# Three PSUM banks instead of two for the up projections of a mixture of experts

## What is computed

```python
x = x + ga * attention(layernorm(x) * (1 + ca) + sa)
h = layernorm(x) * (1 + cb) + sb

def ffn(xt):                                   # xt: the 2048 rows of h
    ew, ei = top_k(xt @ gate_w, 2)
    ew = softmax(ew)
    wE = sum(ew * (ei == each expert))         # (8, tokens), two weights per token
    hid = gelu(einsum('td,edf->etf', xt, w1) + b1)     # 8 experts, 128 -> 256
    o = einsum('etf,efd->etd', hid, w2) + b2           # 256 -> 128
    y = layernorm(xt + o, ln_g, ln_b)                  # one norm per expert
    return einsum('et,etd->td', wE, y)

x = x + gb * ffn(h)
```

## Time and profile before

| | before |
|---|---|
| timed runs, us | 268.58, 270.12, 270.11; median 270.11 |
| profiled execution, us | 268.45, of which 266.7 from the first to the last instruction |
| busy, share of the span | PE 88%, PEld 76%, DVE 69%, ACT 60%, POOL 51% |
| mean granted TensorE clock | 0.976 of full speed |
| the Gelus (line 484) | 128 ACTIVATEs, 50.4 us busy, 472 ns each |

### The profile page before, as it was taken

The page is one execution under the profiler, slowest core; times in us unless marked ns, Lnnn a source line. Parts: engine busy times, 40 slices in busy tenths (PEclk is TensorE's granted clock), DMA queues, the critical chain, the costliest instruction groups (busy, mean ns, idle before and its releaser), DMA issues.

```text
span 266.7 us, 7792 instructions
## 1 busy us (share of the span) xinstructions
PE 235.2 (88%) x3064; PEld 201.8 (76%) x3064; DVE 183.2 (69%) x570; ACT 159.4 (60%) x419; POOL 134.7 (51%) x254
## 2 busy tenths in 40 slices
PE   7796889998999999999999899998999999989970
PEld 3455468887888888888888788887888888858960
DVE  2989858485866677686967587677858595455175
ACT  2454408836695648744893759654884479356650
POOL 8082655247713674266714771367525660378075
PEclk9996899999999999999999999999999999999995
DMA  7930000000000000000000000000000000000000
GB/s 199 366 140 2 2 2 0 2 4 4 0 20 6 0 2 20 4 2 4 20 2 2 0 2 21 5 2 2 20 2 2 2 21 2 4 0 0 22 0 21
DMA packets 5652, 6.23 MB, mean 23 GB/s; under 512 B 336, under 2 KB 5104, under 8 KB 5360
## 3 DMA queue, kind: packets, MB, share of 16 engines
q1 hardware_dynamic: 5616, 5.74, 6.7%
HBM read 4.68 MB, written 1.05 MB: 21 GB/s over the span
## 4 chain that ended last, share of the span: by engine, by line
PE 47%; DVE 24%; ACT 16%; POOL 7%; issue 5%; POOLq 0%; ACTq 0%; DVEq 0%
ACT hid L484 11%; PE z L1003 6%; PE turns L867 6%; PE score L974 6%; DVE q_st L590 6%; PE score L966 5%; ACT L445 3%; DVE ypart L660 3%; PE turns L869 3%; PE turns L868 3%; DVE xn L570 3%; PE score L985 3%; PE score L1048 2%; POOL rstd L340 2%; ACT prob L445 2%
## 5 line engine op out<-in xcount | busy, mean ns | idle before, releaser
L484 ACT ACTIVATE hid<-turns,pack_ffn 128x256 f32<-128x256 f32 x128 | 50.4, 472 | 39.3 <-PE turns L869 39.3
L1003 PEld LDWEIGHTS z<-w,hid 128*128 128x128 f32 x480 | 59.4, 191 | 3.7 <-issue 1.0
L1003 PE MATMUL z<-w,hid 128*128 128x128 f32 x480 | 61.5, 276 | 0.0
L309 POOL TENSOR_SCALAR zvar<-zss 128x4 f32<-128x4 f32 x32 | 6.2, 193 | 78.4 <-DVE zss L646 69.4
L323 POOL TENSOR_TENSOR ypart<-ypart 128x256 f32<-128x256 f32 (+1 forms) x60 | 36.0, 600 | 18.4 <-DVE ypart L660 15.4
L867 PE MATMUL turns<-h_hi,w_hi 128*128 128x256 f32 x128 | 39.7, 310 | 5.0 <-ACT hid L484 4.8
L868 PE MATMUL turns<-h_lo,w_hi 128*128 128x256 f32 x128 | 35.9, 280 | 0.0
L869 PE MATMUL turns<-h_hi,w_lo 128*128 128x256 f32 x128 | 35.9, 280 | 0.0
L660 DVE SCALAR_TENSOR_TENSOR ypart<-z,zcoef,ln_gG 128x128 f32<-128x128 f32 x120 | 34.1, 341 | 1.8 <-POOL zcoef L314 1.7
L310 POOL TENSOR_TENSOR zrstd<-zvar,mhalf 128x4 f32<-128x4 f32 x32 | 33.1, 1033 | 2.7
L867 PEld LDWEIGHTS turns<-h_hi,w_hi 128*128 128x128 f32 x128 | 24.0, 188 | 9.8 <-ACT hid L484 9.5
(11 more groups left out here) (143 smaller groups left out, 454.7 us busy)
## 6 DMA issues: line engine op xcount, KB each, us to landing
w<-in_w SPq DMA_DIRECT2D x2, 1024.0 KB, 7.2
out_x<-yout SPq DMA_DIRECT2D x8, 128.0 KB, 1.8
x_tokens<-in_x SPq DMA_DIRECT2D x1, 896.0 KB, 6.7
ln_g<-in_ln_g SPq DMA_DIRECT2D x1, 512.0 KB
pack_mod<-in_pack_mod SPq DMA_DIRECT2D x1, 385.0 KB, 3.0
pack_proj<-in_pack_proj SPq DMA_DIRECT2D x1, 193.0 KB, 4.3
pack_att<-in_pack_att SPq DMA_DIRECT2D x1, 130.5 KB, 4.2
x_tokens<-in_x SPq DMA_DIRECT2D x1, 128.0 KB, 2.9
```

The costliest lines, as they stand in the source:

```text
L484: last = a.activation(hid[:, e, c, :], U[(e + 1) % 2][:, c * STEP:(c + 1) * STEP], ACT.Gelu, bias=b1[:, e, c:c + 1])
L1003: last = mm(z_bank(f, q)[:, e * D:(e + 1) * D], hid[:, ee, c, tt * P:(tt + 1) * P], w2[:, ee * CH + c, :], start=False, stop=e == HALF - 1 ...
```

## The change

The up projections and the Gelus go round three banks: U[1], U[0] and zB[0], so that up 0, 3 and 6 write U[1], up 1, 4 and 7 write U[0], and up 2 and 5 write zB[0]. In the last step S[0] stands in place of zB[0]. From e = 3 on, up e waits for Gelu e - 3. Up 2 waits until its bank is free of its last reader: in the first step of the sum of biases that was made at the start, in the later ones of the scaling of z 2 of the step before (`u_done`), in the last step of the attention (`x1_s`). z 0, which uses zB[0] again, now also waits for Gelu 5, save in the last step. The first use of U[1] and U[0] in a step, and the last, are by the same experts as before.

The instructions on each engine, and their order, are the same in both kernels.

```diff
+        def up_bank(i, e):
+
+            return (U[1], U[0], S[0] if i == STEPS - 1 else zB[0])[e % 3]
...
                 for c in range(CH):
-                    last = a.activation(hid[:, e, c, :], U[(e + 1) % 2][:, c * STEP:(c + 1) * STEP], ACT.Gelu,
+                    last = a.activation(hid[:, e, c, :], up_bank(i, e)[:, c * STEP:(c + 1) * STEP], ACT.Gelu,
                                         bias=b1[:, e, c:c + 1])
                 last.then_inc(gelu_s, 1)
...
                 if e == 1:
                     pe.wait_ge(g_out, i + 1)
-                if e > 1:
-                    pe.wait_ge(gelu_s, 8 * i + e - 1)
+                if e == 2 and i == STEPS - 1:
+                    pe.wait_ge(x1_s, i + 1)
+                elif e == 2 and i > 0:
+                    pe.wait_ge(u_done, 4 * i - 1)
+                elif e == 2:
+                    pe.wait_ge(bias_o_s, 1)
+                if e > 2:
+                    pe.wait_ge(gelu_s, 8 * i + e - 2)
                 for c in range(CH):
-                    last = three(U[(e + 1) % 2][:, c * STEP:(c + 1) * STEP], w1_hi[:, e, c, :], w1_lo[:, e, c, :],
+                    last = three(up_bank(i, e)[:, c * STEP:(c + 1) * STEP], w1_hi[:, e, c, :], w1_lo[:, e, c, :],
                                  h2_hi[:, i % 2, :], h2_lo[:, i % 2, :])
                 last.then_inc(up_done, 1)
...
                 half, tt = q // 2, q % 2
                 pe.wait_ge(gelu_s, 8 * f + HALF * (half + 1))
+                if f < STEPS - 1 and q == 0:
+                    pe.wait_ge(gelu_s, 8 * f + 6)
```

## The result

The changed kernel took 259.0 us in the median of four runs (257.99, 258.18, 259.82 and 259.93), the kernel before 270.04 beside it (268.58 to 270.12). The ratio is 0.960, with a 95% interval from 0.955 to 0.965: 4% faster. The profiled execution took 257.99 us, 256.2 of it span, against 268.45 and 266.7. The code has become longer at the top, so line 484 is now 488, 867 to 869 are 871 to 873, 974 is 984 and 1003 is 1013.

A forecast was written before the change was run, and what follows sets the result against it. The round of two banks, with TensorE and ScalarE taking turns, was taken as the bound; 7 x 1.33 + 0.99 = 10.30 us, and 269.28 - 10.30 = 259.0 us, range 257.5 to 262.4 us.

The forecast's parts named there:

- The mechanism: Up projections and Gelus: with two banks, up 2 waits for Gelu 0 and Gelu 2 for up 2; gaps of 0.33 us.
- The stage: Gelus of each of the first seven steps: sixteen ACTIVATEs without a gap, 5.95 us in place of 7.28.
- 1.33 per step: Each of the first seven steps: Gelus end 1.33 us sooner, and all of it reaches the next step.
- 0.99 in the last step: Last issue of up 1 to first down projection: 2.96 us at TensorE's pace in place of 3.95, 0.99 less.
- What was priced at nothing: New TensorE waits: up 2 for VectorE's scaling of z, 0.64 us to spare, and down projections for Gelu 5; no cost.
- The level: Timed runs fall on two levels 1.66 us apart: forecast 258.15 and 259.81 us, with the middle taken, 259.0.
- One gap left: Rival: one of three Gelu gaps stays in each of the seven steps, 7.22 us gained, 262.1 us; chance 0.10.
- TensorE as the bound: Rival: TensorE is the bound and only its matmuls' 4.8 us of waiting for Gelus goes, 264.5 us; chance 0.06.
- Given back to VectorE: Rival: the next step waits for VectorE's subtractions, so earlier Gelus gain nothing, 269.3 us; chance 0.03.
- The clock: Rival: the longer gap before the transposes lowers TensorE's clock, 3.0 us in each of seven steps, 280.0 us; chance 0.03.
- Were it 0.25 us shorter, VectorE would be next: VectorE's wait for the small exponential: 1.33 of 1.58 us goes, 0.25 stays as the cover that hides its work.
- TensorE and not ScalarE sets the last step's pace: Last step from up 5 on: down projections stand between the last ups, so TensorE sets the pace.

The follow-up runs named there:

- the kernel with the waits of two: The changed kernel with its three banks, but each up projection from up 2 on again waits for Gelu e-2; 270.49 us, ratio to before 1.003.
- the kernel with two products: The changed kernel without the up projections' product of h with the low part of w1, four matmuls per expert in place of six; 256.62 us, 0.951.
- the kernel with both made quicker: The changed kernel without the product with the low part of w1 and without b1, so one Gelu ACTIVATE per expert; 248.73 us, 0.922.

## Why the prediction was right, and where its steps were not

**The mechanism.** That two banks made TensorE and ScalarE take turns is shown from both sides: the third bank without the later waits gives back all gaps and the time, one wait gives back one gap.

**The terms.** The stage was forecast at 5.95 us and measured 5.96; 1.33 per step against (202.19 - 192.74) / 7 = 1.35; 0.99 in the last step against 1.00, with 2.96 from the last issue of up 1 to the down projection, as worked out. The sum was 10.30, the span lost 10.5 and the profiled execution 10.46. The 0.02 per step that the sum lacks lies in the stage's own two sizes: the Gelus end 5.94 us after the first begins (100.78 - 94.84) and not 5.95, and before they took 7.28 to 7.30 us in the seven steps, of which the sum took the shortest.

**What was priced at nothing** did cost nothing: up 2's wait had 0.63 us to spare (forecast 0.64), the idle time ahead of the transposes is 0.52 (0.53), and 0.24 is left of VectorE's wait (0.25).

**The level.** Both levels came out, 257.99 and 258.18 against 258.15, and 259.82 and 259.93 against 259.81. That two of the four runs fell on each level, so that their median is the forecast middle, is luck: with all four near the upper level, as when the changed kernel ran again, it is 259.4.

**The rivals.** One gap left cost 0.53 per step when it was put back, not 0.44, and did not occur. TensorE as the bound is refuted by the kernel with a third fewer matmuls in the stage, but it is only 0.02 us per expert behind: with a quicker ScalarE it is the bound at once. Given back to VectorE did not happen. The clock stayed at 1.00 in the stage, with stops and without, and in the window of the longer gap. The fall by which that rival was priced did not come again at its place either: in the changed kernel TensorE stood idle for 1.68 us ahead of 22.22, and the windows from 20 to 26 show 1.00. The Trainium skill, page "TensorE: Matmul & The Clock Gate", section "A second HAM failure mode: psum-queue depth-cycling", says that short stops between groups of matmuls that go round PSUM banks make the clock swing; neither kernel shows it in the Gelu stage, before with 23 such stops.

**The step that failed.** "Were it 0.25 us shorter, VectorE would be next" is wrong. Extra work of 1.2 us cost 0.16 per step, so the cover there is about 1.04. The 0.24 was only the first wait on VectorE's row; behind it TensorE takes the weights 0.76 us after they are ready. I had read the cover off the waiting engine's own idle time and not off the engine that waits for its result.

**True by a little** is that TensorE and not ScalarE sets the last step's pace. Gelu 3 ends there at 235.15 and the down projection that needs it starts at 235.50, so TensorE is 0.35 us from being stopped by ScalarE; I had used the statement as if it held for any pace, and with shorter ups the step gained 0.6 where TensorE's alone would have given 1.9.

## What to carry to other kernels

When two engines hand PSUM banks to each other, compare the round trip of all banks (work of both and the two hand-overs) with the slower engine's own pace times the number of banks (here 1.90 us against 2 x 0.73 with two banks): a gap of the same length at every round, and waits of each engine for the other in like number, show that one more bank is worth the gap, up to the slower engine's own pace. A bank that another stage uses will do, if its last reader is done before the round gets there. How much an engine may still grow is read from the consumer of its results, not from its own idle time.

## What the runs showed that was not expected

**A second semaphore on a matmul.** In both kernels in which up 2 waits for two semaphores at once, and the Gelu is the later one, the gap ahead of Gelu 2 is 0.40 us, not 0.33, and the table of waits of the kernel with the waits of two has a row that the kernel before lacks:

```profile
PEld z L871 <- issue: 3.4, 7, 0.5
```

Once in each of seven steps, and its step is 29.14 in place of 29.07. It is not the z bank: in the last step of both kernels up 2 writes S[0], also with two semaphores, and the gap is 0.40 and 0.41. That the second semaphore is the cause was argued from this and not tested by itself.

**TensorE's pace in the first ten microseconds decides the level.** In the thirteen traces here the first Gelu starts either between 39.4 and 39.9 or between 40.6 and 41.1. TensorE's timeline ahead of it, of the changed kernel's first trace

```profile
5.83 1.14 PE L897 MATMUL z<-pack_mod,silu 128*128 128x128 f32 x8
```

and of its second

```profile
6.64 2.05 PE L897 MATMUL z<-pack_mod,silu 128*128 128x128 f32 x8
```

The eight matmuls ahead of these start at 4.94 in both and take 1.02 and 1.84 us. By line 917 (8.87 and 10.20) the second trace is 1.33 us late, and about that it stays up to the first Gelu. All traces fall in line: the same eight matmuls take 1.14 us in the six with the early first Gelu and 2.05 or 2.06 in the seven with the late one. That it is the 1.2 GHz level that makes them slow is argued: the second trace's record of the clock begins only at 12.67, and its windows ahead of that show 1.00 for want of one. But line 917 takes 1.06 us in both traces there, in the first inside the window from 8 to 12 with a clock of 0.57, and 0.70 us later, in windows with 1.00. Why the start is slow in some executions stays open.

**VectorE stood behind GpSimd.** In the first step of the kernel with two products, on VectorE

```profile
41.33 2.79 DVE L701 TENSOR_TENSOR gdif<-gtop 128x2 f32<-128x2 f32 x1
```

and on GpSimd

```profile
41.31 0.45 POOL L367 TENSOR_TENSOR ln_bG<-ln_b,gates 8x128 f32<-8x128 f32 x1
41.73 2.38 POOL L366 TENSOR_TENSOR ln_gG<-ln_g,gates 128x1024 f32<-128x1024 f32 x1
```

A subtraction of two columns, 0.15 us in all other steps, lasted until GpSimd's long operation ended at 44.11, and that step was 28.01 us in place of some 27.5. The trace of the kernel with both made quicker has the same in its first step, 2.81 us, and that step is 28.04 in place of 26.7. The Trainium skill, page "SBUF — State Buffer", section "Who interferes with whom", says that a VectorE instruction with two inputs in SBUF contends with a GpSimd instruction that reads SBUF, and that the order of issue decides who blocks. The rows agree that one stood for the whole operation of the other; but by the record VectorE had started 0.40 us before that operation, while GpSimd's shorter one ran, so the order of the starts alone does not tell why it was VectorE that stood. This was not tested by itself.
